# One block for all stages of a four-layer metaformer kernel, norms that begin inside the stage before, and variances in two layers of rows

## The reference, cut to what matters

```python
def _ln_c(v, eps=1e-06):              # _ln_t is the same over the last axis, eps=1e-05
    m = jnp.mean(v, axis=1, keepdims=True)
    s = jnp.var(v, axis=1, keepdims=True)
    return (v - m) / jnp.sqrt(s + eps)

x = x + conv_i(_ln_c(x))
t = _to_tokens(x)                     # (8, 1024, 64)
t = t + ffn_i(_ln_t(t))
x = _from_tokens(t, x)

# conv_0: batch norm, 1x1 keys, queries and values, linear attention over the pixels
# conv_1: 3x3 convolution whose weights are mixed from 8 sets for each image (16x16 images)
# conv_2: 1x1 to 16 channels, per-image 5x5 and dilated 3x3 taps, 1x1 to 64 channels
# conv_3: 3x3 convolution gives offsets, deformable 3x3, group norm, relu
# ffn_0, ffn_3: 16 experts, hidden 128, top 2 of the softmax:
hidden = silu(x @ w1[e]) * (x @ w2[e]);  out += dispatch[e] * (hidden @ w3[e])
# ffn_1, ffn_2: 8 experts, hidden 256, top 2 of the logits:
h = gelu(x @ W1[e] + b1[e], exact);      out += w_dense[e] * (h @ W2[e] + b2[e])
```

## Time and profile before

| what | us |
|---|---|
| median of 3 runs | 1872.83 (1870.38 to 1875.67) |
| the profiled execution, its own time | 1870.68 |
| its span, first to last instruction | 1868.5 |
| PE busy | 1686.5 (90%) |
| DVE busy | 1100.9 (59%) |
| ACT busy | 977.6 (52%) |
| POOL busy | 879.3 (47%) |

### The profile page before, as it was taken

One profiled execution on the slowest core, in us unless ns is written; L12 is line 12 of the kernel. 1 busy time (PEld: TensorE's weight loads), 2 busy tenths in 40 slices (PEclk: granted clock), 3 DMA queues, 4 the chain that ended last, 5 costly groups with the idle time before them and its releaser, 6 DMA issues. The chain is left out here.

```text
span 1868.5 us, 31745 instructions
## 1 busy us (share of the span) xinstructions
PE 1686.5 (90%) x11879; PEld 947.2 (51%) x11879; DVE 1100.9 (59%) x1526; ACT 977.6 (52%) x1426; POOL 879.3 (47%) x736
## 2 busy tenths in 40 slices
PE   6879999998579999877999977999999759999998
PEld 2635555554234444333444434777777525555554
DVE  5667777765863432365344245656656466777765
ACT  3454555554136666516666643666666445455554
POOL 1418877776024333312333335333333008778777
PEclk8989999999799999999999988999999979999999
DMA  5014333334102322301222230000000004333333
GB/s 119 1 24 104 114 105 108 109 107 129 29 1 77 88 81 78 84 1 28 88 80 66 91 93 1 2 1 2 1 2 1 3 1 116 110 112 122 112 113 98
DMA packets 71584, 121.43 MB, mean 65 GB/s; under 512 B 16962, under 2 KB 18690, under 8 KB 70786
## 3 DMA queue, kind: packets, MB, share of 16 engines
q1 hardware_dynamic: 71426, 119.32, 21.8%
HBM read 115.60 MB, written 3.67 MB: 64 GB/s over the span
## 5 line engine op out<-in xcount | busy, mean ns | idle before, releaser
L675 POOL TENSOR_TENSOR x<-x,mx_gated 128x512 f32<-128x512 f32 x256 | 331.4, 1295 | 94.2 <-DVE mx_gated L630 92.8
L623 DVE TENSOR_TENSOR mx_hidden<-mx_second,mx_hidden 128x1024 f32<-128x1024 f32 (+1 forms) x256 | 245.0, 957 | 179.0 <-PE mx_second L502 179.0
L778 ACT ACTIVATE mx_hidden<-mx_first,w_bias 128x1024 f32<-128x1024 f32 x256 | 264.5, 1115 | 124.8 <-PE mx_first L502 124.8
L821 POOL TENSOR_TENSOR x<-x,mx_gated 128x512 f32<-128x512 f32 x128 | 164.6, 1286 | 260.4 <-DVE mx_gated L795 260.4
L795 DVE SCALAR_TENSOR_TENSOR mx_gated<-mx_out,w_bias,mx_gates 128x512 f32<-128x512 f32 x128 | 96.0, 750 | 286.7 <-PE mx_out L752 265.3
L607 ACT ACTIVATE mx_hidden<-mx_first 128x1024 f32<-128x1024 f32 x256 | 248.6, 1022 | 18.6 <-PE mx_first L502 4.5
L571 PE MATMUL mx_out<-mx_hidden,w_second 128*64 128x512 f32 x1024 | 249.3, 606 | 5.6 <-issue 3.8
L1761 DVE TENSOR_TENSOR c_near_weights<-c_near_hats 128x768 f32<-128x768 f32 x192 | 190.0, 1037 | 103.1 <-PE c_near_turned L1632 103.0
L502 PE MATMUL mx_first<-tokens_high,w_high 64*128 64x512 f32 x1024 | 217.4, 420 | 21.6 <-PEq L64 21.3
L752 PE MATMUL mx_out<-mx_hidden,w_second 128*64 128x512 f32 x1024 | 233.4, 599 | 0.0
L599 ACT COPY mx_kept<-mx_second 128x512 f32<-128x512 f32 x128 | 75.3, 588 | 266.1 <-PE mx_second L502 266.1
(11 more groups left out here) (235 smaller groups left out, 2232.8 us busy)
## 6 DMA issues: line engine op xcount, KB each, us to landing
mx_gates<-gate_board SPq DMA_DIRECT2D x768, 128.0 KB, 3.1
w_first<-in_f_first SPq DMA_DIRECT2D x4, 1024.0 KB, 12.1
c_weight<-in_c_weight SPq DMA_DIRECT2D x1, 2304.0 KB
x<-in_x SPq DMA_DIRECT2D x8, 256.0 KB, 4.7
w_second<-in_f_second SPq DMA_DIRECT2D x4, 512.0 KB, 13.4
w_first<-in_f_first SPq DMA_DIRECT2D x4, 512.0 KB, 10.0
out_x<-x SPq DMA_DIRECT2D x16, 128.0 KB, 2.6
gate_board<-xn SPq DMA_DIRECT2D x16, 64.0 KB, 2.8
```

What stands on the lines that cost most here:

```text
L623: dve.tensor_tensor(own, second[:, 0:halves, :], own, ALU.mult).then_inc(s.hidden.semaphore, 1)
L675: pool.tensor_tensor(place, place, gated[:, n % GATED, :], ALU.add).then_inc(s.added.semaphore, 1)
L778: act.activation(hidden[:, n % HIDDEN, f], first[:, (n * F + f) % BLOCKS], ACT.Gelu, bias=w.bias1[:, e * F + f:e * F + f + 1]).then_inc(s. ...
L821: pool.tensor_tensor(place, place, gated[:, n % GATED, :], ALU.add).then_inc(s.added.semaphore, 1)
```

## The change

1. **One block.** `open_part` opens one block for all stages up to the sampling of conv 3, and a second one from the group norm to the end. The two samplings keep their own. What the barriers ordered is now ordered by waits on semaphores: `ln_normed` by chunk in the convs, `mx_added`, the `added` of each conv, `gt_w_low`, `gt_logits`, `gt_low`, `bn_scaled` by image, `eps_set`. All of PSUM is one tensor `ps`, and stages name banks in it.
2. **Norms begun early.** The first part of norm n+1 (`head_tensor`, `head_scalar`, `head_vector`: four centring products, variances 0, four squares, the square root and reciprocal of pair 0) is issued at the end of the stage before, each product behind a wait for the chunk of `x` that it reads. Since SP has no barrier left to hold it, the transfers that SP issues at an even norm now wait for the last addition of the mixture (`mx_added`).
3. **Two layers of rows.** Variances of a pair are 8 products of 128 moving columns, added up in two layers that use rows 0,1 and 2,3 of a quarter. `ln_dev` and `ln_scale` are 128x128 (in the memory of the gates), and the spreading is 8 products of 128 moving columns with 4 selection matrices. The constants grow from 16 to 32 KB and from 128 to 256 KB.
4. **Order in a norm.** PE's order is variances 1, means 2, spreads 0, variances 2, means 3, spreads 1, (route 0), variances 3, spreads 2, (turns 0, route 1), spreads 3.
5. **Stage edges.** The last step of the swiglu mixture is multiplied wholly on DVE, and the last addition of both mixtures is on DVE. A mixture's first products wait for the split weights, the logits and the low tokens. conv 1 and conv 3 copy each image as soon as it is normalised, conv 2 sums three images on ACT and one on DVE, the batch norm scales by image, and POOL splits weights as soon as they have landed.

```diff
+LAYERS = 2
```

```diff
+    def variances(self, pe, n):
+        k, s = self.k, self.s
+        pe.wait_ge(s.squared, self.chunks + 2 * n + 2)
+        if n >= 1:
+            pe.wait_ge(s.dev, self.pairs + n)
+        for v in range(LAYERS):
+            for q in range(4):
+                last = pe.matmul(self.var[self.quarter(q), 0:self.DEEP], k.averages[:, v, :],
+                                 k.square[:, (2 * n + q // 2) % 4, self.columns(q, v)],
+                                 start=(v == 0), stop=(v == LAYERS - 1))
+        last.then_inc(s.var, 1)
+
+    def spreads(self, pe, n):
+        k, s = self.k, self.s
+        pe.wait_ge(s.scale, self.pairs + n + 1)
+        if n == self.PAIRS - 1:
+            pe.wait_ge(s.kept, self.pairs + n)
+            pe.wait_ge(s.centred, self.pairs + n)
+        elif n >= 1:
+            pe.wait_ge(s.normed, self.chunks + 2 * n)
+        for v in range(LAYERS):
+            for q in (0, 2, 1, 3):
+                last = pe.matmul(self.wide_of(n)[:, q // 2, self.columns(q, v)],
+                                 k.spreading[half(q // 2), q % 2 * LAYERS + v, :],
+                                 k.scale[half(q // 2), n % 2, :], start=True, stop=True)
+        last.then_inc(s.wide, 1)
...
+    def head_tensor(self, pe, ready, start=0, end=4):
+        for i in range(start, end):
+            ready(i)
+            self.centre(pe, i)
+            if i == 2:
+                self.variances(pe, 0)
+
+    def head_scalar(self, act):
+        act.activation(self.k.spare[:, 0:1], self.k.eps[self.eps][:], ACT.Sqrt)
+        self.square(act, 0)
+        self.square(act, 1)
+        self.keep(act, 0)
+        self.square(act, 2)
+        self.deviations(act, 0)
+        self.square(act, 3)
+        self.keep(act, 1)
+
+    def head_vector(self, dve):
+        self.centres(dve, 0)
+        self.centres(dve, 1)
+        self.scales(dve, 0)
+
...
+            elif not router:
+                k.mx.added.wait(sp, 0)
```

The order of the norm on PE, and the mixture's end:

```diff
             if turn == 0:
                 pe.wait_ge(k.constants, k.constants_all)
-            means(0)
-            means(1)
-            variances(0)
+                m.head_tensor(pe, loaded)
+            m.variances(pe, 1)
             means(2)
-            variances(1)
-            variances(2)
-            scales(0)
+            m.spreads(pe, 0)
+            m.variances(pe, 2)
             means(3)
+            m.spreads(pe, 1)
             if router:
-                variances(3)
-                scales(1)
                 route(0)
-                scales(2)
+            m.variances(pe, 3)
+            m.spreads(pe, 2)
+            if router:
                 turns(0)
                 route(1)
-                scales(3)
+            m.spreads(pe, 3)
+            if router:
                 turns(1)
                 route(2)
                 route(3)
                 turns(2)
                 turns(3)
-            else:
-                scales(1)
-                variances(3)
-                scales(2)
-                scales(3)
             if turn == 0:
...
-            if e == 0 and n // E >= EARLY:
+            if n == 0:
+                pe.wait_ge(k.gt.w_low, k.w.pieces)
+                pe.wait_ge(k.gt.logits, top_two.PAIRS * (k.mixtures + 1))
+            if e == 0:
                 pe.wait_ge(k.gt.low, lows(k, n // E))
...
+        def ready(i):
+            s.act.wait(pe, STEPS - 1 if i < HALVES else STEPS)
+            s.added.wait(pe, E * (i + 1))
+
+        if following:
+            following.head_tensor(pe, ready, 0, 1)
         second_layer(STEPS - 1)
         third_layer(STEPS - 2)
+        if following:
+            following.head_tensor(pe, ready, 1, 2)
         third_layer(STEPS - 1)
+        if following:
+            following.head_tensor(pe, ready, 2, 4)
 
     @block.scalar
     def _(act):
...
+    def add_last(self, dve, x, gated):
+        steps = CHUNKS * self.E
+        self.s.gated.wait(dve, steps)
+        self.s.added.wait(dve, steps - 1)
+        place = x[:, chunk(CHUNKS - 1)]
+        dve.tensor_tensor(place, place, gated, ALU.add).then_inc(self.s.added.semaphore, 1)
...
-        keep(STEPS - 1)
+        if following:
+            following.head_scalar(act)
```

The convs, the batch norm and the blocks:

```diff
+                if c % 2 == 0:
+                    pe.wait_ge(k.bn.scaled, c // 2 + 1)
...
+        for j in range(IMAGES):
+            image = xn[:, j * PIX:(j + 1) * PIX]
+            dve.tensor_scalar(image, image, both[:, 5:6], both[:, 7:8], ALU.mult, ALU.add).then_inc(s.scaled, 1)
...
+                act.wait_ge(k.ln.normed, normed + 2 * (j + 1))
                 act.copy(padded[:, j, 1:1 + H, 1:1 + W], image[:, j]).then_inc(s.padded, 1)
...
-            for c in range(2):
-                for j in range(IMAGES):
-                    last = pe.matmul(f_ps[j * Q:(j + 1) * Q, c, :], w[:],
+            for j in range(IMAGES):
+                pe.wait_ge(k.ln.normed, normed + max(2 * (j + 1), CHUNKS - 2))
+                for c in range(2):
+                    last = pe.matmul(f_ps[c][j * Q:(j + 1) * Q, :], w[:],
                                      xn[:, j * PIX + c * BANK:j * PIX + (c + 1) * BANK], start=True, stop=True)
...
+            for j in range(IMAGES - 1):
+                scratch = (near[:].rearrange("p y x -> p (y x)"), by_both[:].rearrange("p t c -> p (t c)"),
+                           by_near[:].rearrange("p t c -> p (t c)"))[j]
+                act.wait_ge(k.ln.normed, normed + 2 * (j + 1))
                 act.activation(scratch[:, 0:PIX], xn[:, j * PIX:(j + 1) * PIX], ACT.Copy,
                                accum_out=total[:, j:j + 1]).then_inc(s.other_total, 1)
...
+            dve.tensor_reduce(total[:, IMAGES - 1:IMAGES], xn[:, N - PIX:N], AX.X, ALU.add).then_inc(s.total, 1)
...
-                pe.wait_ge(s.high, r + 1)
-                pe.wait_ge(s.padded, r + 1)
+                pe.wait_ge(s.high, r + 2)
+                if r == 1:
+                    pe.wait_ge(s.padded, 1)
...
+def open_part(k):
+    k.block = k.part.enter_context(k.nc.Block(no_gpsimd_drain=True))
```

The selection matrices:

```diff
-    spreading = np.zeros((2, 2, P // 4, 2, HALVES, C), np.float32)
-    for q in range(2):
+    averages = np.zeros((HALVES, C, LAYERS, P // 4), np.float32)
+    spreading = np.zeros((2, 2, P // 4, 2, LAYERS, HALVES, C), np.float32)
+    for v in range(LAYERS):
         for h in range(HALVES):
-            spreading[:, q, h, q, h] = 1
-    c["spreading"] = spreading.reshape(P, 2, P)
+            averages[h, :, v, HALVES * v + h] = 1.0 / C
+            for q in range(2):
+                spreading[:, q, HALVES * v + h, q, v, h] = 1
+    c["averages"] = averages.reshape(P, LAYERS, P // 4)
+    c["spreading"] = spreading.reshape(P, 2 * LAYERS, P)
     p = "L0_conv_"
     c["c0_wk"] = diagonal(f(p + "wk").T)
```

481 lines of the change are left out of this document (253 added, 228 removed).

## The result

The changed kernel takes 1824.2 us in the median of 4 runs (1823.78 to 1826.13), the kernel before 1874.25 (1870.38 to 1878.24). The ratio is 0.9731, with a 95% interval from 0.9711 to 0.9751: 50 us less. Forecast were 1828 and a range from 1812 to 1850. The profiled executions differ by 46.5 us in their spans (1868.5 and 1822.0), where the sum of the prediction was 44.9. In two later groups of runs the same kernel took 1827.2 and 1824.3.

The account below looks back on a forecast made before the run. PE, the busiest engine, was taken to bound the kernel, with time to gain where it waits at stage edges, in norms and at conv starts. Terms summed to -44.9 us, so 1825.8, put at a median of 1828, range 1812 to 1850.

Parts of the forecast that it names:

- the 1.4 for the branches: Stages are still jumps: 19 branches at an estimated 0.07 us each, adding 1.4 us to the sum.
- rival 2: Halved products cost by column and the clock stays up through all heads: 1816 us, chance 0.13.
- the loss of 1.2: Norms beside a router: root of pair 3 stands behind later variances 3, so 21.1 us instead of 19.9, in each of four.
- The term of +1.4: Turns 0 and batch norm: norm and barrier gains outweighed by 3.7 us of DVE operations slowed beside POOL's early split.
- my two norm terms: Turns 0 and batch norm: first norm gains about 1.3 us inside, and the two barriers after it give 1.
- Turn 1: Second norm and first mixture, -1.7 us: centring 1.1 earlier, norm loses 1.2, mixture start through the gates gives 1.8.
- the sign that the prediction named for being wrong: In a norm: a window showing a clock under 1.00 after the norm's first 3 us.
- Turn 4: Fifth norm and conv 2, -10.4 us: norm ends 5.3 earlier, taps ready 3.45 after it, giving 5.1.
- Turn 6: Seventh norm and offsets, -12.8 us: norm 6.3, offsets starting with the last image's chunks 3.1, higher clock kept 3.4.
- Rivals 1 and 4: 1: halved products cost by pass, 1848 us, chance 0.17; 4: heads don't begin early, 1859 us, chance 0.06.
- Rival 5: PE drops to the lower clock inside the norms: 1916 us, or 1872 in half of them; chance 0.04.
- rival 3: POOL locks out all seven DVE operations in batch norm (+3), and again at conv 2's taps (+5): 1836 us, chance 0.12.

Follow-up runs that it names:

- e3: Changed kernel with its part closed and opened again at stage edges, putting 16 barriers back: 1849.80 us, ratio 0.9878.
- e4: Changed kernel with each norm's first centring product waiting until all of x is added, no barriers: 1848.21 us, ratio 0.9867.
- e8: The changed kernel itself, nothing edited, timed again for comparison: 1827.21 us, ratio 0.9743 to the kernel before.
- e1: Changed kernel with one layer of rows again (reciprocal 128x256, products of 256 columns): 1823.84 us, ratio 0.9735.
- e5: Changed kernel with POOL's first split of weights waiting until the batch norm has scaled all four images: 1821.46 us, ratio 0.9724.
- e7: Changed kernel with spare PE products at the start of each mixture (ten in swiglu, six in gelu): 1819.59 us, ratio 0.9712.
- e6: Changed kernel with spare PE products before four small results of conv 0 and before conv 2's taps: 1821.27 us, ratio 0.9721.
- e2: Kernel before with the two layers of rows alone, its blocks and order kept: 1869.58 us, ratio 0.9982.

## Why the prediction was right

**The mechanism and its size.** The gain was put down to the edges between stages, each worked out from idle time of PE, and all nine stretches of the table came within 1.7 us of their terms. e3 and e4 bear it out: barriers back cost 25.6 by the medians and 25.3 by the spans, and heads that wait for all of `x` 24.0 and 18.5. No run has both edits, so whether the two shares add up isn't shown. The sum was 1.6 us too small against the profiled span. That it was so near is in part luck: the terms missed by +1.55, +0.97, -0.4, -1.0, +0.7, -1.6, +0.5 and -0.8, the 1.4 for the branches was not found, and these nearly cancel; and another execution of the same kernel (e8) has a span 5.0 longer than the one in the table.

**The prices of the halved forms** were too high where I chose between bounds. The spreading was set at 1.35, from the overlap of four loads, with 1.14 as the lower bound: measured 1.16. The variances were set at 0.75: measured 0.64 to 0.65. That is the price of rival 2, by columns alone, and the chain of an even norm, which I had at 18.3 (rival 2 at 17.2), took 17.74 from the first centring product to the last multiplication at turns 4 and 6. The reciprocal was 0.947 for the 0.95 worked out from two rows. The rule of the Trainium skill that spoke against me ("TensorE: Matmul & The Clock Gate", section "LDWEIGHTS (loading the stationary operand)") would have made it an estimated 1.7. With 64-row weights that lie in alternating halves the trace doesn't show that: the 16 loads take 0.97 us in all, 0.06 each. Each norm was therefore shorter than my chain: beside a router the loss of 1.2 didn't come (20.2 from 521.31 to 541.53 at turn 3, for 19.9 before), and these 0.9 are the larger part of the 1.0 and 1.6 by which turns 3 and 5 came out better. One reading of the rows before was wrong without a place in the sum: not the first seven but the first four centring passes of the fifth norm ran at the lower clock.

**The reciprocal beside PE's products.** That the shorter reciprocal "lies mostly beside them" held: e1 shows that with 1.75 instead of 0.95 only 0.33 comes on the path of an even norm and 0.05 on that of an odd one at turns 3 and 5. That PE's slower products would then take back a part was the wrong half of the same sentence.

**Turns 0, batch norm and conv 0.** The term of +1.4 was +2.95. The mechanism stood in it, DVE locked out by POOL, at 3.7 for the small operations. From the aggregate of the statistics to the start of the scaling it is 5.84 us in the changed kernel and 2.92 in e5, so the small operations cost 2.9. The early split cost 4.7 in all at the end of the keys, and the part that I had left out is the clock: PE's longer wait left it down for the first key products, 1.7 us. Without POOL's early split the keys end 3.95 before those of the kernel before (43.15 and 47.10), where my two norm terms said 2.3. Up to the end of the keys the term came out 0.6 better than forecast (+0.8 for +1.4). The miss lies behind them, in the clock that falls before the small products of conv 0 and not behind them, about 2.2 (L1017 and L1023 1.92 and 2.36 us for 1.06 and 1.39). No rival had it, and it isn't there in every execution: in e1 the clock falls behind these products, and conv 0 takes 49.16 from the end of the keys, as before (49.20), for 51.35. The Trainium skill's rule ("SBUF — State Buffer", "Who interferes with whom") agrees with the rows of the small operations, up to 1.19 for 0.16, and it names the scaling's form too, which took 6.74 for 2.98; I had applied it to the small ones only. That second part didn't cost time here, since PE waited for the first image alone.

**Turn 1.** -0.73 for -1.7. PE's first expert products stand at 122.82, but DVE's choice of the top two begins when the last logits are there, 2.9 later than before. The norm's tail ran at 0.50 in the window 117 to 120. This is the sign that the prediction named for being wrong, a lower clock in a norm after its first 3 us; it showed in one norm of this execution, where it cost some 0.6 (9.54 from the last centring product to the end, for 8.92 at turns 3, 5 and 7), and at turn 5 in e7 (10.47). So the gates came at 129.88 instead of 127.28. PE then waited 4.75 us and came out at the lower clock; e7 shows that this alone was worth 2.4 at the first product of the second layer and 2.1 at the second transposition of gates.

**Turn 4.** -9.7 for -10.4. I had POOL's split end near 798 in the old count, 3 before the norm's end; it ended at 786.84, 4.0 behind it, and the first tap still took 0.94. The other three (there are four such operations, not the five that I counted) were short, as forecast (0.22 to 0.30). The taps were ready 4.8 after the norm and not 3.45, which is more than the term missed.

**Turn 6.** -12.3 for -12.8, and the clock stayed at 1.00 at the start of the offsets:

```profile
1078.00:1080.00 2.00, 2.00 (x43) 0.79 (x48) 1.97 (x5) 1.05 (x1) 0.00 (x0) 1.00 0.91 195
```

**Rivals.** Rivals 1 and 4 fell. Rival 5 fell too as a cause of the time: in this execution the clock is up throughout the norms of turns 2 to 6, and the one tail at turn 1 cost 0.6. Rival 2 was right in its prices, rival 3 in its mechanism; their effects were of opposite sign, and the time came out between.

**What stays open.** The clock in conv 0 was mended only in part by spare products, and why it falls where it does isn't shown. In the profiled e1, e5, e6 and change it falls at different products, which is also my reading, not shown, of why the runs of e5 and e8 spread by 6.9 and 8.5 us.

## What to carry to other kernels

Price an edge between stages by what the barrier keeps from overlapping on every engine: here it was 25 us for 16 barriers, and at conv 2, where the rows are shown, the next stage's first copies, splits and products are the larger part. A shorter link in a chain gives little if another engine's work covers it, so ask for each link who waits for it (e1, e2). Freeing an engine from a barrier moves its work onto others: POOL's split, set free early, made DVE's small operations longer and PE's wait with them, and after that wait PE's next products ran at the lower clock, 4.7 us in all; one wait on POOL gave it back. Before a small gain is put down to an edit, look at the same stretch in the traces of the kernels that don't have the edit: 0.7 in conv 2 and 0.8 in a gelu mixture turned up there too.

## What the runs showed of the hardware

- Products with 64-row, 128-column weights in alternating halves cost by moving columns: 16 passes of 128 columns take 1.16 us, 8 of 256 take 1.13; with 32-column weights in four quarters 0.64 and 0.64.
- A tensor_scalar of 128x1024 in SBUF takes 0.75 us alone (2.98 for four) and 1.7 beside POOL's two-input operations (6.74 for four), and POOL's take 1.71 there, instead of 1.26 for those beside the small operations (11.62 for eight of both kinds, 9.90 where they lie elsewhere).
- The granted clock stood at 0.61 and 0.54 in two windows in which PE was busy for all of 2 us, with small and spare products (e6, 84 to 88 us): being busy there didn't bring it back at once. It was 1.00 in the two windows that follow, 88 to 92.
